# A place for every step in each of seven classes of groups: one hand-written order replaced by another

## The reference

```
x0, x1 = pairs of neighbouring rows of x                  # rotation by a per-sequence angle
r = rotate(x; a**delta_t * cos, a**delta_t * sin)
xn = layernorm(r) * ln_g + ln_b
for xn forward and for xn reversed:                       # mamba, DI=256, N=16 states
    xi, z = split(xn @ in_proj.T)
    u = silu(causal_conv4(xi));  dt, B, C = split(u @ x_proj.T)
    delta = softplus(dt @ dt_proj.T + b)
    h_t = exp(delta_t * A) * h_(t-1) + delta_t * u_t * B_t        # per channel and state
    y = (sum over states of h * C + u * D) * silu(z)
y = gelu([y_forward, y_backward] @ fused out/reduce weights)
x = x + r + glu(y)
h = relu(x @ W1[expert of the sequence]);  c = h @ W2[expert]     # LoRA merged into the weights
f = silu(c @ w1) * (c @ w2);  f = gelu(f @ h1);  f = gelu(f @ h2)
return x + f @ w3
```

## Time and profile before

| | us |
|---|---|
| median of 3 runs | 1058.82 |
| lowest and highest run | 1056.62, 1059.22 |
| span of the profiled execution, first to last instruction | 1057.0 |
| TensorE busy | 944.2 (89%) |
| VectorE busy | 920.4 (87%) |
| GpSimd busy | 855.6 (81%) |
| ScalarE busy | 779.4 (74%) |
| mean granted TensorE clock | 0.953 |

### The profile page before, as it was taken

How to read it: one execution, slowest core, us unless ns; L and a number is a source line. 1 busy time by engine, 2 the same in 40 slices (tenths; PEclk the granted TensorE clock), 3 DMA queues, 4 the chain that set the end, 5 groups by cost and what they waited for, 6 DMA issues and landing times.

```text
span 1057.0 us, 13719 instructions
## 1 busy us (share of the span) xinstructions
PE 944.2 (89%) x4320; PEld 603.2 (57%) x4320; DVE 920.4 (87%) x722; ACT 779.4 (74%) x1241; POOL 855.6 (81%) x428
## 2 busy tenths in 40 slices
PE   4698688879989999999999999989889987998897
PEld 3455456656645566555755575546655575556556
DVE  1988999999999999999999999898999999978701
ACT  4858767878598868987788869886687867777522
POOL 0777999989987998989897999899788898866400
PEclk9797699889999999999999999999999998999999
DMA  3855655673556645755456464664646564555100
GB/s 114 285 177 198 203 164 165 178 210 103 181 166 189 190 130 150 239 146 169 164 178 202 117 190 154 194 178 130 158 134 184 159 187 130 142 172 150 39 1 16
DMA packets 97670, 167.43 MB, mean 158 GB/s; under 512 B 9920, under 2 KB 33408, under 8 KB 97344
## 3 DMA queue, kind: packets, MB, share of 16 engines
q1 hardware_dynamic: 97600, 166.57, 52.6%
HBM read 159.19 MB, written 7.34 MB: 158 GB/s over the span
## 4 chain that ended last, share of the span: by engine, by line
PE 44%; ACT 17%; issue 16%; DVE 14%; POOL 8%; DMA 1%; SPq 0%; DVEq 0%; POOLq 0%; ACTq 0%
DVE bank_d L980 9%; PE bank_y L1274 9%; PE bank_m L1104 8%; PE bank_m L1180 7%; POOL state L595 5%; PE bank_m L1187 5%; ACT bank_d L745 4%; ACT L626 4%; PE bank_m L1153 3%; DVE state L978 2%; POOL state L600 2%; PE bank_m L1194 2%; PE bank_m L1162 2%; PE bank_m L1169 2%; PE bank_m L1122 1%
## 5 line engine op out<-in xcount | busy, mean ns | idle before, releaser
L595 POOL TENSOR_TENSOR state<-du,b_rows 128x1024 f32<-128x1024 f32 (+1 forms) x288 | 629.1, 2210 | 53.6 <-PE bank_y L1274 46.1
L980 DVE TENSOR_TENSOR_SCAN bank_d<-bank_d,state 128x1024 f32<-128x1024 f32 (+1 forms) x225 | 461.2, 2050 | 32.0 <-ACT bank_d L745 30.9
L745 ACT ACTIVATE bank_d<-delta,a_neg 128x512 f32<-128x512 f32 (+1 forms) x540 | 322.6, 634 | 78.2 <-DVE state L985 73.5
L1274 PEld LDWEIGHTS bank_y<-ident,state 128*128 128x128 f32 x2048 | 243.9, 147 | 92.5 <-issue 63.4
L1274 PE MATMUL bank_y<-ident,state 128*128 128x128 f32 x2048 | 270.2, 284 | 25.9 <-DVE gated L996 12.5
L985 DVE TENSOR_TENSOR state<-bank_d,c_rows 128x1024 f32<-128x1024 f32 (+1 forms) x225 | 248.8, 1106 | 7.7
L600 POOL TENSOR_TENSOR state<-state,c_rows 128x1024 f32<-128x1024 f32 (+1 forms) x63 | 134.1, 2128 | 16.7 <-DVE state L978 15.7
L1104 PE MATMUL bank_m<-xnT,w_conv 128*128 128x508 f32 (+7 forms) x288 | 118.4, 557 | 4.5 <-DVE x1T L1005 2.4
L1187 PE MATMUL bank_m<-hidA,h_s 128*128 128x512 f32 (+1 forms) x256 | 112.5, 585 | 5.7 <-ACT hidA L817 4.6
L1180 PE MATMUL bank_m<-hidB,h_s 128*128 128x512 f32 (+1 forms) x256 | 107.8, 573 | 0.8 <-DVE hidB L1019 0.8
L978 DVE TENSOR_TENSOR_SCAN state<-bank_d,state 128x1024 f32<-128x1024 f32 (+1 forms) x45 | 92.0, 2044 | 3.4 <-ACT bank_d L745 3.4
(11 more groups left out here) (152 smaller groups left out, 1047.6 us busy)
## 6 DMA issues: line engine op xcount, KB each, us to landing
b_rows<-bc_store SPq DMA_DIRECT2D x256, 256.0 KB, 5.0
c_rows<-bc_store SPq DMA_DIRECT2D x256, 256.0 KB, 4.7
wsel<-merged SPq DMA_DIRECT2D x32, 512.0 KB, 3.5
...
```

The lines of the kernel that those rows point to most:

```text
L595: nc.gpsimd.tensor_tensor(split(unit_state(u)), du[:, d, :, :width(g)], per_half(b_rows, u), ALU.mult).then_inc(S.bx_ready, 1)
L745: ins = act.activation(split(unit_decay(u))[:, h], delta[:, d, h, :width(g)], ACT.Exp, scale=a_neg[:, h, n:n + 1])
L980: dve.tensor_tensor_scan(decay, decay, drive, 0.0, ALU.mult, ALU.add).then_inc(S.scanned, 1)
L1274: ins = pe.matmul(bank_y[:, h, s * P:(s + 1) * P], split(unit_state(u))[:, h, s * LEN:(s + 1) * LEN], ident[:, :], start=(n == 0 and s == ...
```

## The change

Each step gets a place of its own for each of seven classes of groups (`STAGE`: groups 0, 1 and 2 are classes 0 to 2; 3, 4 and 5 share class 3; 6, 7 and 8 are classes 4 to 6). The tables hold tuples of seven, the four tables of shifts go, every take has a lag of its own, and nearly all numbers are new. The program of each engine otherwise stays as it is: the same steps, each with the same waits. The load of the back weights (`load_back`, now BACK_AT) stays at 3.0. The core of the diff:

```diff
+STAGE = (0, 1, 2, 3, 3, 3, 4, 5, 6)
-FILL = {"norm": -25.5, "uf0": -23.0, "uf1": -21.0, "ur0": -23.5, "ur1": -19.0, "z0": -18.5, "z1": -18.5, "dbc0": -9.5,
-        "dt00": -9.0, "dt01": -8.5, "dbc1": -2.0, "dt10": -0.5, "dt11": 1.0, "out": 37.5, "glu1": 38.5, "glu0": 42.0,
...
+        "dbc0": (-34, -11, -10, -10, -10, -10, -10),
+        "dt00": (-16.5, -9, -10, -8.5, -9.5, -9, -9),
+        "dt01": (-18.5, -9.5, -10, -8, -9, -9.5, -9.5),
...
+        "h1_0": (59.5, 56.5, 56.5, 57.5, 57.5, 56.5, 71.5),
+        "h1_1": (58.5, 57, 57, 54.5, 57, 56, 69.5),
+        "h1_2": (56, 55, 58, 58.5, 54.5, 57, 73),
+        "h1_3": (59.5, 59, 57, 57.5, 57.5, 58.5, 73),
+        "h2_0": (65.5, 65.5, 68, 65, 63, 67, 78.5),
...
+        "w3": (71, 72.5, 71, 71, 70.5, 77.5, 85),
+        "tok": (72.5, 73.5, 73, 73.5, 72, 95, 87.5)}
+SETUP = {"fuse": -12.5, "wi0": -12.5, "wo0": 4.5, "wi1": -13, "wo1": 7, "wi2": 11, "wo2": 11, "wi3": 14,
+         "wo3": 19, "wi4": 20.5, "wo4": 20.5, "wi5": 24, "wo5": 22.5, "wi6": 27.5, "wo6": 28, "wi7": 29,
+         "wo7": 28.5}
-TAKE_LAG = {"uf0": 1.5, "uf1": 1.5, "ur0": 1.0, "ur1": 2.5, "dbc0": 0.5, "dbc1": 0.5, "h1_0": 0.5, "h1_1": 0.5,
-            "h1_2": 1.5, "h1_3": 2.0, "h2_0": 0.5, "h2_1": 0.0, "h2_2": -4.0, "h2_3": 0.5, "out": 1.0, "wo": 2.5}
-ACT_AT = {"scale": -36.5, "normalise": -27.5, "softplus": (-6.0, 4.0), "copied": (18.5, 32.5), "front": -10.5,
-          "silu": 52.0, "skip": (12.5, 24.5), "sigmoid": 42.0, "gelu": (61.5, 70.5)}
...
+            "hid0": (-69, -141.5, -85.5, -94.5, -45.5, -107, -137),
+            "hid1": (-29, -51, -46, -36, 1, 0.5, 6),
+            "hid2": (1.5, -31.5, 0.5, 2, 1.5, 2.5, -18.5),
+            "hid3": (-30, -73, -59, 2, -17, -12.5, -47),
...
+            "h1_0": (-44, 1, -36, 1.5, 1.5, 0, 3),
+            "h1_1": (-5, 3.5, 2.5, 1, 1, 2, -36.5),
+            "h1_2": (3, 0.5, 3, 2.5, 0.5, 10, -10.5),
+            "h1_3": (2.5, -14, -5, -9.5, -53.5, 4, -3.5),
...
+ACT_AT = {"scale": (-32, -33.5, -35.5, -36, -41.5, -36.5, -35),
+          "normalise": (-9.5, -27.5, -30.5, -29, -27, -27, -27),
+          "softplus": ((-8.5, -5, -7.5, -5.5, -6.5, -6, -7), (8.5, 6.5, 1.5, 0.5, 0.5, 0.5, -1.5)),
+          "copied": ((18.5, 18, 19, 19, 18, 17.5, 18.5), (31.5, 32.5, 32.5, 34, 33.5, 34, 43.5)),
+          "front": (2, -10, -11.5, -10, -10.5, -10.5, -11),
+          "silu": (51, 51.5, 53.5, 52, 50.5, 52.5, 33),
+          "skip": ((-1, 19.5, 18.5, 35, 18.5, 12, 9.5), (42, 51.5, 63.5, 57.5, 58.5, 29.5, 23.5)),
+          "sigmoid": (41.5, 43, 40, 41.5, 40, 43, 45),
+          "gelu": ((63, 61.5, 61.5, 61.5, 60.5, 69, 97.5), (70.5, 69.5, 70, 69.5, 71.5, 82, 109.5))}
-VEC = {"rotate": -31.5, "gated": (20.5, 36.0), "x1": 44.5, "up0": 53.0, "up1": 53.5, "up2": 54.5, "up3": 54.5,
-       "w3": 74.0}
-GPS = {"power": -32.5, "residual": -11.5, "delta": (-4.0, 5.0), "inputs": (-3.5, 8.0)}
+VEC = {"rotate": (-14, -29, -31.5, -31.5, -34.5, -32.5, -32.5),
+       "gated": ((21.5, 20.5, 20, 21, 21, 19, 20), (35.5, 35, 34.5, 36, 36, 36, 46.5)),
+       "x1": (43, 43.5, 44, 44.5, 43.5, 44.5, 52),
+       "up0": (52, 53, 54, 53.5, 52.5, 54.5, 87.5),
...
+       "w3": (72.5, 74, 73, 73, 74.5, 95, 94)}
+GPS = {"power": (-28.5, -27.5, -30.5, -33, -32.5, -28, -28),
+       "residual": (-37.5, -11.5, -12, -14, -20.5, -12, 0.5),
+       "delta": ((-3, -4, -5.5, -5, -4, -4.5, -4.5), (7.5, 10.5, 7, 5.5, 2, 4, 5.5)),
+       "inputs": ((-22.5, -4, -5, -3.5, -3.5, -4.5, -4.5), (12.5, 11.5, 12.5, 11, 9, 4.5, 10.5))}
-LOADS = {"x": -40.0, "bc_store": (-7.5, -1.0), "selected": (23.5, 26.5, 28.5, 31.0), "store": 76.0, "back": 3.0}
+         "selected": ((38, 20, 24, 27.5, 16, 16, 17), (38, 35, 26.5, 31, 20.5, 27, 27.5), (54.5, 36.5, 43, 32.5, 23.5, 31.5, 32.5), (61, 43, 44, 33.5, 37, 39.5, 36.5)),
+         "store": (75.5, 79, 78, 75.5, 76.5, 79.5, 74)}
...
-            last = max(last, UNITS * g + slot(FILL, g, name) + TAKE_LAG.get(name, 1.0))
+            last = max(last, UNITS * g + slot(FILL, g, name) + slot(TAKE_LAG, g, name))
...
-    shifts = {0: FIRST_GROUP, 1: SECOND_GROUP, NG - 2: NEXT_TO_LAST, NG - 1: LAST_GROUP}.get(g, {})
-    return at + shifts.get(name, 0.0) + (0.0 if k is None else shifts.get(f"{name}:{k}", 0.0))
+    return (table[name] if k is None else table[name][k])[STAGE[g]]
```

More of the change, by code:

```diff
@@ L66 @@
-ACT_AT = {"scale": -36.5, "normalise": -27.5, "softplus": (-6.0, 4.0), "copied": (18.5, 32.5), "front": -10.5,
-          "silu": 52.0, "skip": (12.5, 24.5), "sigmoid": 42.0, "gelu": (61.5, 70.5)}
-DECAY_LEAD = 2
-VEC = {"rotate": -31.5, "gated": (20.5, 36.0), "x1": 44.5, "up0": 53.0, "up1": 53.5, "up2": 54.5, "up3": 54.5,
-       "w3": 74.0}
-GPS = {"power": -32.5, "residual": -11.5, "delta": (-4.0, 5.0), "inputs": (-3.5, 8.0)}
+FILL = {"norm": (-47, -26.5, -28, -26.5, -26.5, -26.5, -25.5),
[12 rows of a table added]
+        "out": (38, 36.5, 37, 37.5, 37.5, 37, 36.5),
+        "glu1": (40.5, 40.5, 39.5, 38, 38.5, 38.5, 37),
+        "glu0": (42, 41.5, 41.5, 41.5, 41.5, 41, 37),
+        "res": (42.5, 41.5, 42.5, 41.5, 42.5, 42, 39.5),
[22 rows of a table added]
+        "tok": (72.5, 73.5, 73, 73.5, 72, 95, 87.5)}
@@ new lines @@
+SETUP = {"fuse": -12.5, "wi0": -12.5, "wo0": 4.5, "wi1": -13, "wo1": 7, "wi2": 11, "wo2": 11, "wi3": 14,
+         "wo3": 19, "wi4": 20.5, "wo4": 20.5, "wi5": 24, "wo5": 22.5, "wi6": 27.5, "wo6": 28, "wi7": 29,
+         "wo7": 28.5}
+MERGE_LAG = 2
+TAKE_LAG = {"norm": (38.5, 1, -35.5, -24, -12, -10.5, -1.5),
[12 rows of a table added]
+            "out": (2, -10, 1.5, 1, 0.5, 2.5, -7),
[18 rows of a table added]
+            "tok": (-14, -25.5, -1, -81, -75, -63, -70.5)}
+ACT_AT = {"scale": (-32, -33.5, -35.5, -36, -41.5, -36.5, -35),
[7 more added lines that the diff above has]
+          "gelu": ((63, 61.5, 61.5, 61.5, 60.5, 69, 97.5), (70.5, 69.5, 70, 69.5, 71.5, 82, 109.5))}
@@ L80 @@
 TURN = (19.0, 36.0)
-LOADS = {"x": -40.0, "bc_store": (-7.5, -1.0), "selected": (23.5, 26.5, 28.5, 31.0), "store": 76.0, "back": 3.0}
-ROW_LEAD, C_LEAD = 6, 3
-FIRST_GROUP = {"ur1": 5.5, "h1_1": -2.0, "h2_0": 0.0, "power": -3.5, "bc_store": 1.0, "ur0": 10.0, "z0": 6.5, "z1": 8.5,
[5 rows of a table removed]
-               "w3": 0.5, "gate1": -1.0, "delta": -1, "inputs": 0, "normalise": -1.0, "gated": 0.5, "back": 2,
[3 rows of a table removed]
-LAST_GROUP = {"up0": 2.5, "uf1": 5.5, "h2_2": 9.5, "delta": -1, "ur0": 1.0, "h2_0": 18.0, "h2_1": 21.0, "h2_3": 10.0,
[4 rows of a table removed]
-              "scale": 0.5, "glu1": -1.0, "store": 5.5, "norm": 0, "back": 2.5, "selected:2": 5.0, "gated:1": -1.5,
[4 rows of a table removed]
-SECOND_GROUP = {"scale": 4.0, "rotate": 2.5, "power": 3.0, "residual": -3.0, "back": 3, "store": 4, "z0": 4.5, "hid3": 2,
[7 rows of a table removed]
-NEXT_TO_LAST = {"res": 0.0, "residual": -2.5, "copied": 0.5, "h2_1": 4.5, "glu0": 0.0, "hid1": 1.5, "ur1": -1.0, "store": -5,
[7 rows of a table removed]
+LOADS = {"x": (-71, -38.5, -46, -44.5, -42.5, -41, -47),
+         "bc_store": ((-26.5, -7, -9, -8.5, -8.5, -8.5, -9), (8.5, 4.5, 1.5, 6, 1.5, -0.5, 0.5)),
+         "selected": ((38, 20, 24, 27.5, 16, 16, 17), (38, 35, 26.5, 31, 20.5, 27, 27.5), (54.5, 36.5, 43, 32.5, 23.5, 31.5, 32.5), (61, 43, 44, 33.5, 37, 39.5, 36.5)),
+         "store": (75.5, 79, 78, 75.5, 76.5, 79.5, 74)}
+BACK_AT = 3.0
+ROW_LEAD, C_LEAD = 6, 3
 FIRST, STEP, END = -48.0, 0.5, 96.0
@@ L156, in slot @@
 def slot(table, g, name, k=None):
-    at = table[name] if k is None else table[name][k]
-    shifts = {0: FIRST_GROUP, 1: SECOND_GROUP, NG - 2: NEXT_TO_LAST, NG - 1: LAST_GROUP}.get(g, {})
-    return at + shifts.get(name, 0.0) + (0.0 if k is None else shifts.get(f"{name}:{k}", 0.0))
+    return (table[name] if k is None else table[name][k])[STAGE[g]]
 def first_pair(g):
@@ L524, in _ @@
                     load_c(u)
-                if at == LOADS["back"]:
+                if at == BACK_AT:
                     load_back()
```

3 lines of the change are left out of this document (removed), and 83 rows, old and new, of tables (FILL, FIRST_GROUP, LAST_GROUP, NEXT_TO_LAST).

## The result

The changed kernel takes 1034.46 us (median; 1032.83 to 1036.62) beside 1058.99 us of the kernel before on the same chip: a ratio of 0.9773, 95% interval 0.9751 to 0.9796. The gain is 24.5 us; the record said 13.8 (1045), with a low end of 1035.

The account below looks back on a forecast made before the run. VectorE and TensorE were taken to share the limit. Middle steps -12.6, cut to -8.4 by TensorE, with head -3 and end -3 made -14.4: span 1042.6, median 1044.4, rounded to 1045 us; range 1035 to 1060.

Parts of the forecast that it names:

- (f): End: group 7's up-products behind unit 278, two h1 takes behind the last decay; -3 us, bounds -6 and +3.6.
- (e): Head: merges and fused-weights copy ahead of the first inputs, -1; reordered merges and front fills, -2; bounds -8 and +3.
- (a): Rotate of groups 6, 7, 8 moves ahead of units 158, 192, 224, shrinking three boundary stalls; -5.1 us, bounds -5.6 and +1.5.
- (d): Slow group (from 683.5): normalise ahead of decay 199, w3 ahead of the conv fills; -2 us, bounds -4 and +1.
- TensorE returns a third: Middle groups: TensorE, with 4.95 us idle, takes back a third of the -12.6 us gain, leaving -8.4.
- rotate near 2.2: Sign for the rotate move: no wait before units 160, 192, 224, and rotate still takes about 2.2 us.
- (b): First-pass gate of groups 3 to 6 moves behind one more scan, covering its waits; -3 us, bounds -4.4 and +0.4.
- (c): First h1 fill moves ahead of the first-pass dt fills, freeing decays 155, 187, 219; -2.5 us, bounds -3.5 and +1.5.
- The quarter of VectorE's idle time: Head up to 107.7 us: new order of merges and front fills wins a quarter of 9.0 us idle, taken as -2.
- stalls that only move: Rival: the next decay is late by what the last was not; no change, 1059 us, chance 0.08.
- Clustered takes ahead of decays: Rival: rows of takes ahead of decays wait for TensorE and stall scans, +22 us against -12 left; 1068, chance 0.12.
- The rotates that stand beside GpSimd's products: Rival: early scans and rotates meeting GpSimd products lengthen, +12.5 us, eating the gain; 1057, chance 0.06.

Follow-up runs that it names:

- the run with the h2 takes back: Changed kernel with the four h2 fills of group 6 and their takes in the old order again; ratio 0.9792, last group 70.2 us.
- the two filled runs: Extra matmuls put into TensorE's waits: in the kernel before (slow group 683.5 to 807.6), ratio 0.9999; in the changed kernel with h1 back, 0.9947.
- h1 back: Changed kernel with the first h1 fill of groups 3 to 5 behind the dt fills again, its take ahead of decays 155, 187, 219; 1053.67 us, ratio 0.9950.

## Why the prediction was too small

The step that failed is the size of (f), put at -3: the last group and the tail gave 9.0, and these stretches repeat. Its premise was that TensorE rules the end and works off the same instructions there. But the last group has 306 matmuls of TensorE instead of 334 (63.43 us busy instead of 71.47): nine matmuls of the h2 fills of group 6, whose move the prediction put at nothing, run a group earlier, and 17 transposes fall into the tail. The last group is 10.4 us shorter, of which the run with the h2 takes back shows 3.3, and the tail returns only 1.4. Beside it (e), also -3, was too small, by 4.6 in this pair of profiles and by some 2 between the middles of all. That the total for (a) to (d) came out near is luck: its entries did not.

- **What bounds it**: right for VectorE (its idle time up to the last scan went from 85.0 to 51.7 us) and for TensorE beside it (10.4 and 13.6 of 17.6 us added came through). "TensorE returns a third" took 4.2 us off, and nothing shows that reordering pays so: the new order also put TensorE's work into TensorE's own waits, so that it is busy for 927.7 instead of 944.2 us on the same instructions at a granted clock of 0.975 instead of 0.953. By the two filled runs the clock itself makes at most a third of the loss in the slow group before, and at most half in groups 4 and 5 with h1 back.
- **(a)** -5.1: undone, 5.1 in the stretches. Its sign "rotate near 2.2" failed (3.15, 3.65, 3.35). The rule of the Trainium skill weighed there (SBUF — State Buffer, "SBUF: two separate sides") put 2 to 6 us on the new place. That isn't borne out as a price of the move, since rotate is as long in the old place once the rest is new.
- **(b)** -3: 3.4, but in group 3 alone; elsewhere another wait was ready to take its place.
- **(c)** -2.5: the entry furthest from what undoing it costs, 19 us. Its size was read from the wait that it removes, which is about right for it alone (2.4). The record saw `scale` move ahead of decay 153 and priced it at 0.7, as a step of its own. In group 4 the two are a pair by the timelines, and 9.1 of the 24.2 us lost in that profile lie there; for groups 5 and 6 the cause stays open.
- **(d)** -2: normalise alone 3.9. Group 6 came out at 114.2, the 114 that was forecast, but only together with group 7.
- **(e)** -3: the head gave 7.6 by unit 96 in this pair of profiles, within the bounds, and 4.7 between the middles of twelve and three executions. The quarter of VectorE's idle time was a guess and too low. The merges, the one part that was worked out, can't be told from no effect.
- **(f)** -3: last group and tail gave 9.0, beyond the bound of -6. The h2 takes of group 6 (3.3) weren't in the list, the up-products are worth 1.1, the h1 takes 2.9 less 2.1 handed on to the tail. If these add up, some 3.8 us are not attributed.
- **Sum**: by place, the middle (groups 3 to 7) gave 9.8 against 8.4 forecast, although 4.6 of unit 104's scan work against it; (e) and (f) were short by 4.6 and 6.0, and that is the miss. By edit, the parts undone add up to over 30 us: they can't be summed. (The sum on record comes to 1044.4; it was put down as 1045.)
- **The rivals**: stalls that only move explains (b), not the whole. Clustered takes ahead of decays didn't cost on the whole; waits for decays fell by 18 us. The rotates that stand beside GpSimd's products grew, by 8.4 us in all; early scans grew at units 104 and 232 and shrank at 81, 209 and 241; together they take 48.0 us, as before (48.2).
